# Attention and feed-forward layer on one core: causal mask folded into the row-minimum operation on VectorE, gate columns merged with the value projection, half of the odd pairs' scaling on ScalarE, and a new order on all engines

## The reference

```
h = layernorm(x) * (1 + ca) + sa
x = x + ga * attention(h)
h = layernorm(x) * (1 + cb) + sb
x = x + gb * ffn(h)

attention(h): r = rmsnorm(h); q, k, v = r @ Wq, r @ Wk, r @ Wv     (16 heads of 64)
    p = softmax(mask_causal(q @ k.T / 8)); gate = sigmoid(r @ Wg)   (one column for each head)
    return (gate * (p @ v)) @ Wout
ffn(h): mlp = (silu(h @ Wg + bg) * (h @ Wu + bu)) @ Wd + bd
    scores of 4 retrieval heads against 2 x 64 keys, the 8 best of each, the 8 best sums, softmax over them
    experts = sum of silu(h . down[i]) * weight[i] * up[i] over the chosen of 512 experts
    return mlp + experts
```

## Time and profile before

| | us |
|---|---|
| median of 3 runs | 1555.74 |
| lowest and highest | 1555.52, 1555.81 |
| the profiled execution's own time | 1555.38 |
| its span, first to last instruction | 1553.6 |
| TensorE busy in the span | 1480.7 (95%) |
| VectorE busy | 1347.4 (87%) |
| ScalarE busy | 1142.6 (74%) |
| GpSimd busy | 1098.7 (71%) |

### The profile page before, as it was taken

One profiled execution on the slowest core, in us unless ns is written; L12 is line 12 of the kernel. 1 busy time (PEld: TensorE's weight loads), 2 busy tenths in 40 slices (PEclk: granted clock), 3 DMA queues, 4 the chain that ended last, 5 costly groups with the idle time before them and its releaser, 6 DMA issues.

```text
span 1553.6 us, 39532 instructions
## 1 busy us (share of the span) xinstructions
PE 1480.7 (95%) x12385; PEld 1194.9 (77%) x12385; DVE 1347.4 (87%) x3993; ACT 1142.6 (74%) x3687; POOL 1098.7 (71%) x1203
## 2 busy tenths in 40 slices
PE   4899999999999999999999999999999999999963
PEld 2577888787888878788887878888787888878753
DVE  4579998989999998999999899999989999998874
ACT  2677777887777788777778877777887777788731
POOL 2027787777778777777877777787777778777677
PEclk7899999999999999999999999999999999999976
DMA  4000000000000000000000000000000000000000
GB/s 126 18 14 18 14 23 22 22 17 15 20 14 22 22 22 15 17 18 16 22 22 22 15 17 17 17 22 22 22 15 17 16 18 22 22 22 8 12 12 9
DMA packets 46126, 32.01 MB, mean 21 GB/s; under 512 B 5680, under 2 KB 41328, under 8 KB 45968
## 3 DMA queue, kind: packets, MB, share of 16 engines
q1 hardware_dynamic: 45856, 31.20, 7.2%
q10 hardware_dynamic: 240, 0.43, 0.1%
HBM read 27.31 MB, written 4.31 MB: 20 GB/s over the span
## 4 chain that ended last, share of the span: by engine, by line
PE 90%; DVE 5%; POOL 2%; ACT 2%; issue 1%; DMA 0%; POOLq 0%; ACTq 0%; DVEq 0%
PE pS L1029 11%; PE pW L964 11%; PE pW L965 10%; PE pW L966 10%; PE pW L1045 9%; PE pS L1018 7%; PE pS L1014 7%; PE pW L1069 6%; PE pW L1105 4%; PE pW L1108 4%; PE pS L1020 3%; PE pW L1049 3%; PE pS L1021 2%; PE pW L1097 2%; POOL fexp L421 1%; PE pW L978 1%
## 5 line engine op out<-in xcount | busy, mean ns | idle before, releaser
L529 ACT ACTIVATE pS<-pS,nmx 128x128 f32<-128x128 f32 (+1 forms) x1024 | 390.4, 426 | 33.5 <-DVE nmx L728 30.9
L421 POOL TENSOR_TENSOR fexp<-fexp,fsum 128x512 f32<-128x512 f32 x256 | 342.1, 1373 | 64.9 <-DVE fexp L864 64.9
L745 DVE TENSOR_TENSOR p_sb<-pS,coef 128x256 f32<-128x256 f32 (+1 forms) x512 | 261.7, 552 | 8.9
L412 POOL TENSOR_TENSOR fsum<-ex 128x512 f32<-128x512 f32 x256 | 258.3, 1047 | 0.0
L521 ACT COPY pT<-pS 128x768 f32<-128x768 f32 x256 | 212.5, 848 | 19.5 <-PE pS L1029 19.5
L1029 PE MATMUL pS<-ident,p_sb 128*128 128x128 f32 x1536 | 217.4, 278 | 8.5 <-DVE p_sb L745 8.4
L1029 PEld LDWEIGHTS pS<-ident,p_sb 128*128 128x128 f32 x1536 | 171.4, 141 | 28.5 <-issue 16.3
L864 DVE TENSOR_SCALAR fexp<-fsum,top,rz 128x512 f32<-128x512 f32 x256 | 192.1, 813 | 1.2
L727 DVE TENSOR_REDUCE nmx<-pS 128x2 f32<-128x256 f32 x256 | 108.3, 423 | 91.2 <-PE pS L1021 84.9
L529 ACT ACTIVATION_READ_ACCUMULATOR pS<-pS,nmx 128x1 f32 x1024 | 185.7, 181 | 0.0
L728 DVE TENSOR_REDUCE nmx<-pS 128x2 f32<-128x512 f32 x256 | 174.1, 680 | 0.0
(11 more groups left out here) (178 smaller groups left out, 3923.1 us busy)
## 6 DMA issues: line engine op xcount, KB each, us to landing
modB<-mods_dram SPq DMA_DIRECT2D x32, 256.0 KB, 3.2
x_in<-in_L_attn_tokens SPq DMA_DIRECT2D x32, 128.0 KB, 2.1
modA<-mods_dram SPq DMA_DIRECT2D x32, 128.0 KB, 3.1
x_res<-in_L_attn_tokens SPq DMA_DIRECT2D x32, 128.0 KB, 3.0
out<-yo SPq DMA_DIRECT2D x32, 128.0 KB, 1.9
...
```

The costliest lines, as they stand in the source:

```text
L412: ins = nc.gpsimd.tensor_tensor(fsum[:, k, h], ex[:, k, h, 0:NX].unsqueeze(2).broadcast_to([P, NX, NK]), ex[:, k, RH + h, :].unsqueeze(1). ...
L421: ins = nc.gpsimd.tensor_tensor(fexp[:, k, h, :], fexp[:, k, h, :], fsum[:, k, h].rearrange("p i j -> p (i j)"), ALU.mult)
L529: ins = nc.scalar.activation(ps, ps, ACT.Exp, bias=nmx[:, p % 2, h, k:k + 1], accum_out=den(p)[:, h, k:k + 1])
L745: ins = nc.vector.tensor_tensor(p_sb[:, p % 2, :, cols_of(k)], pS[:, p % 2, :, cols_of(k)], coef[:, :, k:k + 1].broadcast_to([P, 2, (k + 1 ...
```

## The change

1. **Mask.** The four mask matmuls of each pair go. `mask` becomes a 128 x 256 float32 tile, 128 columns of zero and 128 of the triangle. `row_max` becomes four `tensor_tensor_reduce` operations, one for each head and block, each over 128 or 256 columns: they write -(s + mask) back to `pS` in place and give its minimum to `nmx`. `exp_scores` gets scale -1.
2. **Gate with the values.** The weights are laid out as q, k, gate, v. V has six tiles: for each 128 tokens 16 gate columns and heads 0 to 3 (272 columns), heads 4 to 9 (384) and heads 10 to 15 (384). `project_gate` goes; `values` takes the tanh of 16 columns ahead of the copy of tiles 0 and 3.
3. **Odd pairs.** In pairs 1, 3, 5 and 7 VectorE scales head 0 alone, and ScalarE head 1 (`scale_head`, two activations), when `coef` is there. `coef` has two buffers. The transposes of these pairs wait for both.
4. **Second layernorm.** Lines 825 and 826 go; ScalarE applies scale 1 + cb and shift sb after the transposition, in PSUM (`modulate_h`), from a tile `col` of two values for each partition. SyncE loads `col` (128 partitions x 8 bytes) after the residual of x, behind a wait for `h2T_high` of the batch before. `modB` holds two vectors in place of four.
5. **Similarities.** `shift(k)` takes the eight largest of each group from PSUM (eight MAX8) in place of the one largest, and subtracts the first; one operation of 128 elements makes `top_d`, ScalarE takes its exponential as `tops`, and `sim_tops` goes.
6. **Feed-forward product.** Both halves of y share one bank; `finish` is two operations of 256 columns in place of four of 128.
7. **Order.** The `pW` list still has 36 products (V 6, y 1, no gate). The new orders:

The core of the diff (order lists, constant set-up and renamed indices left out):

```diff
+if w.live(-1):
+    sp.wait_ge(S(h2T_high), at(h2T_high, i - 1, 1))
+sp.dma_start(col[:, :], mods_dram[bass.ds(i, 1), COL * D:(COL + 2) * D].rearrange("o (d m) -> d (o m)", m=2)).then_inc(S(col_loaded), 16)
-w.wait_released("y", 1)
+w.wait_released("y")
...
-                ins = nc.scalar.activation(ps, ps, ACT.Exp, bias=nmx[:, p % 2, h, k:k + 1], accum_out=den(p)[:, h, k:k + 1])
+                ins = nc.scalar.activation(ps, ps, ACT.Exp, bias=nmx[:, p % 2, h, k:k + 1], scale=-1.0, accum_out=den(p)[:, h, k:k + 1])
+def scale_head(p):
+    if w.live(0):
+        act.wait_ge(S(coef_ready), at(coef_ready, i, p + 1))
+        for k in range(TB):
+            ins = nc.scalar.activation(p_sb[:, p % 2, 1, cols_of(k)], pS[:, p % 2, 1, cols_of(k)], ACT.Copy, scale=coef[:, p % 2, 1, k:k + 1])
+        ins.then_inc(S(p1_ready), 1)
...
-k, half = divmod(n, 2)
-evacuate(v[:, k, half * BANK:(half + 1) * BANK], w.bank("V", n)[:, :], "V", n)
+k, c = divmod(n, NV)
+heads = slice(VCUT[c] * DH, VCUT[c + 1] * DH)
+w.wait_full("V", n)
+bank = w.bank("V", n)
+first = 0
+if c == 0:
+    first = H
+    if k == 0 and w.live(-1):
+        act.wait_ge(S(coef_ready), at(coef_ready, i - 1, NP))
+    nc.scalar.activation(g_th[:, k, :], bank[:, 0:H], ACT.Tanh, scale=0.5)
+w.release(nc.scalar.copy(v[:, k, heads], bank[:, first:first + heads.stop - heads.start]), "V", n)
...
-                     ACT.Exp).then_inc(S(ex_ready), 1)
+                     ACT.Exp)
+if k == TB - 1:
+    act.wait_ge(S(top_d_ready), at(top_d_ready, f, 1))
+    if w.live(-2):
+        act.wait_ge(S(cand_ready), at(cand_ready, g, 1))
+    nc.scalar.activation(tops[:, :, :, :].rearrange("p a h n -> p (a h n)"), top_d[:, :, :, :].rearrange("p a h n -> p (a h n)"),
+                         ACT.Exp).then_inc(S(tops_ready), 1)
...
+if w.has("hT"):
+    w.wait_full("hT")
+    act.wait_ge(S(col_loaded), at(col_loaded, f, 16))
+    o = w.bank("hT")[:, 0:N]
+    nc.scalar.activation(o, o, ACT.Identity, bias=col[:, 0:1], scale=col[:, 1:2]).then_inc(S(h2T_mod), 1)
...
-nc.vector.reduce_max(nmx[:, s % 2, :, 0], pS[:, s % 2, :, 0:P], AX_X, negate=True)
-nc.vector.reduce_max(nmx[:, s % 2, :, 1], pS[:, s % 2, :, P:SW], AX_X, negate=True).then_inc(S(max_ready), 1)
+apart()
+for h in range(2):
+    for k in range(TB):
+        ps = pS[:, s % 2, h, cols_of(k)]
+        ins = nc.vector.tensor_tensor_reduce(out=ps, in0=ps, in1=mask[:, (1 - k) * P:2 * P], scale=-1.0, scalar=LARGEST,
+                                             op0=ALU.add, op1=ALU.min, accum_out=nmx[:, s % 2, h, k:k + 1])
+ins.then_inc(S(max_ready), 1)
-    w.wait_released("gate")
+    w.wait_released("V", 0)
+    w.wait_released("V", NV)
-ins = nc.vector.scalar_tensor_tensor(out=coef[:, :, :], in0=g_th[:, :, 2 * p:2 * p + 2].rearrange("p k h -> p h k"),
+ins = nc.vector.scalar_tensor_tensor(out=coef[:, p % 2], in0=g_th[:, :, 2 * p:2 * p + 2].rearrange("p k h -> p h k"),
+ins.then_inc(S(coef_ready), 1)
+dve.wait_ge(S(coef_ready), at(coef_ready, i, p + 1))
-    ins.then_inc(S(coef_ready), 1)
-    dve.wait_ge(S(coef_ready), at(coef_ready, i, 1))
-else:
-    link(ins, attn_chain, i)
+mine = slice(0, 1) if p in SHARED else slice(0, 2)
-    ins = nc.vector.tensor_tensor(p_sb[:, p % 2, :, cols_of(k)], pS[:, p % 2, :, cols_of(k)],
-                                  coef[:, :, k:k + 1].broadcast_to([P, 2, (k + 1) * P]), ALU.mult)
+    o = p_sb[:, p % 2, mine, cols_of(k)]
+    ins = nc.vector.tensor_tensor(o, pS[:, p % 2, mine, cols_of(k)],
+                                  coef[:, p % 2, mine, k:k + 1].broadcast_to(o.shape), ALU.mult)
...
-        link(ins, head_chain, f)
-        link(nc.vector.tensor_tensor(h2[:, :, :], h2[:, :, :], modB[:, 1:2, :].broadcast_to([P, TB, D]), ALU.mult), head_chain, f)
-        nc.vector.tensor_tensor(h2[:, :, :], h2[:, :, :], modB[:, 0:1, :].broadcast_to([P, TB, D]), ALU.add).then_inc(S(h2_ready), 1)
+        ins.then_inc(S(h2_ready), 1)
-        sim = w.bank("sim", k)[:, :].rearrange("p (g n) -> p g n", n=NK)
-        link(nc.vector.reduce_max(top1[:, k, :], sim, AX_X), head_chain, f)
-        w.release(nc.vector.tensor_tensor(sh[:, k, :, :], sim, top1[:, k, :].unsqueeze(2).broadcast_to([P, 2 * RH, NK]),
-                                          ALU.subtract), "sim", k)
+        sim = w.bank("sim", k)[:, :].rearrange("p (a h n) -> p a h n", a=2, n=NK)
+        heads = slice(k * RH, (k + 1) * RH)
+        apart()
+        for a in range(2):
+            for h in range(RH):
+                ins = nc.vector.max(top_s[:, a, k * RH + h, :], sim[:, a, h, :])
+        link(ins, head_chain, f)
+        w.release(nc.vector.tensor_tensor(sh[:, k].rearrange("p (a h) n -> p a h n", a=2), sim,
+                                          top_s[:, :, heads, 0:1].broadcast_to([P, 2, RH, NK]), ALU.subtract), "sim", k)
+            nc.vector.tensor_tensor(top_d[:, :, :, :], top_s[:, :, :, :], top_s[:, :, :, 0:1].broadcast_to([P, 2, TB * RH, TK]),
+                                    ALU.subtract).then_inc(S(top_d_ready), 1)
-def sim_tops(k):
-    if w.live(-1):
-        dve.wait_ge(S(ex_ready), at(ex_ready, f, k + 1))
-        apart()
-        for j in range(2 * RH):
-            ins = nc.vector.max(tops[:, j // RH, k * RH + j % RH, :], ex[:, k, j, :])
-        ins.then_inc(S(tops_ready), 1)
...
-def finish(k):
-    if w.has("y", k):
-        w.wait_full("y", k)
+def finish():
+    if w.has("y"):
+        w.wait_full("y")
-        o = w.bank("y", k)[:, 0:D]
-        nc.vector.tensor_tensor(o, o, modC[:, 0, :], ALU.mult).then_inc(S(y_gated), 1)
-        dve.wait_ge(S(y_gated), at(y_gated, g, k + 1))
-        if k == 0:
-            dve.wait_ge(S(x2g_ready), at(x2g_ready, g, 1))
-            if w.live(-3):
-                dve.wait_ge(S(out_stored), at(out_stored, g, 0))
-        w.release(nc.vector.tensor_tensor(yo[:, k, :], o, x2g[:, k, :], ALU.add), "y", k)
+        o = w.bank("y")[:, 0:N].rearrange("p (k d) -> p k d", k=TB)
+        nc.vector.tensor_tensor(o, o, modC[:, 0:1, :].broadcast_to([P, TB, D]), ALU.mult).then_inc(S(y_gated), 1)
+        dve.wait_ge(S(y_gated), at(y_gated, g, 1))
+        dve.wait_ge(S(x2g_ready), at(x2g_ready, g, 1))
+        if w.live(-3):
+            dve.wait_ge(S(out_stored), at(out_stored, g, 0))
+        w.release(nc.vector.tensor_tensor(yo[:, :, :], o, x2g[:, :, :], ALU.add), "y")
...
-        k, half = divmod(n, 2)
+        k, c = divmod(n, NV)
+        lo = GV + (H + VCUT[c] * DH if c else 0)
+        hi = GV + H + VCUT[c + 1] * DH
-        w.filled(mm3(w.bank("V", n)[:, :], cols(xT, k * P, (k + 1) * P),
-                     cols(s_qkv, 2 * DI + half * BANK, 2 * DI + (half + 1) * BANK)), "V", n)
-def project_gate():
-    if w.has("gate"):
-        w.wait_free("gate")
-        for k in range(TB):
-            ins = mm3(w.bank("gate")[:, k * H:(k + 1) * H], cols(xT, k * P, (k + 1) * P), cols(s_gate, 0, H))
-        w.filled(ins, "gate")
+        w.filled(mm3(w.bank("V", n)[:, 0:hi - lo], cols(xT, k * P, (k + 1) * P), cols(s_qkv, lo, hi)), "V", n)
...
-    mm(ps[:, h, 0:P], qk[r, p % 4, 0:P], qk[r, p % 4, N:N + P], start=True, stop=False, skip_group_check=True)
+    mm(ps[:, h, 0:P], qk[r, p % 4, 0:P], qk[r, p % 4, N:N + P], start=True, stop=True, skip_group_check=True)
-    mm(ps[:, h, P:SW], qk[r, p % 4, P:N], qk[r, p % 4, N:2 * N], start=False, stop=False, skip_group_check=True)
-for h in range(2):
-    mm(ps[:, h, 0:P], ident_bf[:, :], mask[:, :], start=False, stop=True, skip_group_check=True)
-    ins = mm(ps[:, h, 2 * P:SW], ident_bf[:, :], mask[:, :], start=False, stop=True, skip_group_check=True)
+    ins = mm(ps[:, h, P:SW], qk[r, p % 4, P:N], qk[r, p % 4, N:2 * N], start=False, stop=True, skip_group_check=True)
...
-if p == 0:
-    w.wait_released("V", 2, i)
-    w.wait_released("V", 0, i)
-if p == NP // 2:
-    w.wait_released("V", 1)
-    w.wait_released("V", 3)
+if 2 * p in VCUT:
+    for k in range(TB):
+        w.wait_released("V", k * NV + VCUT.index(2 * p))
```

More of the change, by code:

```diff
@@ L33 @@
 SCALE = float(DH) ** -0.5
+GV = 2 * DI
+VCUT = (0, 4, 10, H)
+NV = len(VCUT) - 1
 LN_EPS = 1e-5
@@ L99, in program @@
         modA = sb("modA", [P, 2, D])
-        modB = sb("modB", [P, 4, D])
+        modB = sb("modB", [P, 2, D])
+        col = sb("col", [P, 2])
         modC = sb("modC", [P, 1, D])
@@ L883, in body @@
                 thresholds()
+                row_max(0)
                 choose(0, 0)
                 choose(0, 1)
-                choose(1, 0)
-                row_max(0)
-                choose(1, 1)
                 row_max(1)
-                gated_down(0)
                 normalise(0)
-                ln1_stats()
-                normalise(1)
-                ln2_stats()
                 bias_product(1)
                 gate_product(1)
+                normalise(1)
+                gated_down(0)
@@ L897, in body @@
+                choose(1, 0)
+                gated_down(1)
                 row_max(2)
-                gated_down(1)
+                row_max(3)
```

(27 more changed lines are left out.)

220 lines of the change are left out of this document (110 added, 110 removed), and 10 rows, old and new, of the table order.

## The result

The median falls from 1555.78 us to **1514.33** (four runs each), a ratio of 0.9735 (95% interval 0.9718 to 0.9752): 41 us faster. The forecast was 1469, a gain of 87; the range (1452 to 1515) holds the result by less than 1 us at its far end. So the direction was right and the size was not: less than half of the forecast gain came.

The account below looks back on a forecast made before the run. TensorE was taken as the bound, at 45.38 us a period; -2.96 gave 42.42, plus 0.25 idle 42.67. The 2.71 saved, times 32, is 86.7 off 1555.4: 1469 us, range 1452 to 1515.

Parts of the forecast that it names:

- TensorE, -2.96 us, packed period 42.42: TensorE, one iteration: mask -2.64, gate product -0.59, V tiles +0.09, order +0.18, giving 42.42 us if packed.
- 1.10 a pair: VectorE's row_max: minima taken at 0.21 us for 128 columns and 0.34 for 256, 1.10 a pair against 0.94.
- the in-place write to PSUM costs nothing: VectorE's row_max: writing the result back to PSUM adds no time, as SBUF and PSUM operations run at one rate.
- don't overlap: Rival at row_max: the four minima run their whole durations, 1.74 us a pair, time 1577; chance 0.07.
- half rate: Rival at row_max: two inputs and the accumulator halve the minimum's rate, +6.3 us on VectorE, time 1607; chance 0.03.
- busy 38.97, with the small gaps 40.7: VectorE, one iteration: changes sum to -2.27, busy 38.97 us; 1.7 of small gaps make 40.7, below TensorE's 42.4.
- 0.25 us of idle TensorE: Added waits: TensorE allowed 0.25 us idle per iteration, between nothing and the second rival's 1.5.
- h2: two operations of 0.42 go: -0.84: VectorE's second layernorm: removing two operations of 0.42 us saves 0.84 us an iteration.
- Hand-offs cost more: Rival: scale_head 0.3 us late each, exp 3 and tops 0.15 each; 1.5 us idle per iteration, time 1509; chance 0.32.
- Against it: TensorE lost nothing with VectorE full to 95%: Argument against the 1509 us hand-off rival: in the kernel before, TensorE had no idle time despite VectorE's load.
- the signs of being wrong: Prediction wrong if row_max's block exceeds 1.3 us, holes precede transposes 3, 5 or scores 3, or 0.33 us stays after scores.
- forecast 39.4: ScalarE, one iteration: scale_head, modulate_h, tops, V copies and tanh add 3.9 us, making 39.4 of 42.4.

Follow-up runs that it names:

- experiment 7: Changed kernel with the mask back on TensorE (four matmuls and two reductions a pair), rest of the change kept: 1545.28 us, 0.9935 of the kernel before.
- experiment 11: Changed kernel with h2's two VectorE operations given an unread accumulator output, multiplication by the reciprocal deviation left out: 1484.63 us, ratio 0.9553.
- experiment 15: Changed kernel with h2 complete on VectorE in two accumulator-form passes, mean then reciprocal deviation: 1481.83 us, 0.9532 of the kernel before.
- 11 to 14: Changed kernel with accumulator-form h2, 1484.63 us; h1 too, 1485.12; plus gate product 2 and y0 earlier, 1487.07; or h2 on GpSimd, gate product 2 earlier, 1510.47.

## Why the prediction was right in sign and wrong in size

- **TensorE, -2.96 us, packed period 42.42: right within half a microsecond.** The estimate from the runs is 41.9, and the agreement of 42.41 in experiment 7 is in part chance. The spacings of V (0.12 to 0.13 and 0.17 to 0.18), the gate's absence and the change from scores to the next product (0.53, so the 0.33 of the mask is gone whole) came as forecast. One thing that the sum left out: where scores follow scores, the two changes of kind around the mask go as well (0.43 and 0.22 in place of 0.53 and 0.33 between scores 6 and 7).
- **row_max, "1.10 a pair": mis-sized,** 1.22 to 1.26, about 1.1 us an iteration. The rows that I used, L794, have 128 columns; both start 0.21 apart from what follows. The minimum does so for the first of a group only, and its accumulator read lasts 0.14 in place of 0.08. Where the 0.04 more for each operation comes from is open: "the in-place write to PSUM costs nothing" rested on rows that don't write to PSUM, and no run separates it. No bound of the forecast was passed: 1.31 was where VectorE would decide, and the rivals "don't overlap" (1.74) and "half rate" are refuted.
- **VectorE, "busy 38.97, with the small gaps 40.7": this step failed,** and with it the allowance "0.25 us of idle TensorE", which measured about 2.2. It priced each operation by its duration in a row of before, whatever ran beside it. "h2: two operations of 0.42 go: -0.84" counted only what went; the two that stay had moved beside weigh 1, since I had walked the new order of GpSimd for x2g and modB but not for what VectorE does meanwhile. They grew from 340 to 1201 ns, and `top_d` cost 1.35 in place of 0.21. Of the 2.2 us, 1.0 hangs on h2 alone (44.13 to 43.14, experiment 11); the 32 us of experiment 15 are seven tenths of the 45 us between forecast and result.
- **"Hand-offs cost more" (1509):** its time came close, and partly by chance, since TensorE's own work is less and its idle time more than the rival had (1.5 us). About half of the idle time is not of its kind: the holes ahead of h2's transposes and sim 0 come from the blocked operations. The other half is a matter of late hand-offs and orders, but at other places than most of those listed: none ahead of transposes 3 or 5, where I had put scale_head's lateness, and 0.3 to 0.4 at scores 3, which was on the list and among the signs of being wrong. "Against it: TensorE lost nothing with VectorE full to 95%" was a poor argument: how full an engine is says nothing about which of its results is late.
- **ScalarE** 38.6 of the forecast 39.4. No wait of TensorE for modB, `col` or x2g appears, so these steps held.

What stays open: the best version still loses about 1.2 us an iteration (43.12 against 41.9), of which 0.35 ahead of QK4, where TensorE waits for gate product 2, 0.24 ahead of ET1, and 0.37 at scores 3; making gate product 2 earlier cost time elsewhere (11 to 14). A `top_d` that doesn't wait, with h2 in the new form, wasn't tried.
